# A third slot for the probabilities of attention, in the memory of the spread weights, and a wider search for TensorE's order

## The reference

```python
# layer 0: one attention head of width 128 with a causal mask, and 16 experts of width 64, two of them chosen per token
x = x + attn0(xn, R) + moe0(xn)
xn = layernorm(x)
# layer 1, first part: 16 heads of width 8, no mask
scores = einsum('bhqd,bhkd->bhqk', q, k) / sqrt(8)
ctx = einsum('bhqk,bhkd->bhqd', softmax(scores), v)
# layer 1, second part: 16 heads of width 4 on a projection to 64, causal, then 8 experts of width 256, two per token
scores = where(causal, einsum('bhqd,bhkd->bhqk', rope(q), rope(k)) / sqrt(4), -inf)
x = x + out(ctx) + moe1(x + up(softmax(scores) @ v))
```

## Time and profile before

| | before |
|---|---|
| median of 3 runs | 1917.72 us |
| lowest and highest | 1913.46 and 1918.71 us |
| the profiled execution | 1918.81 us |
| its span | 1917.0 us |
| PE, DVE, ACT, POOL busy | 1791.3, 1339.1, 1214.5, 373.6 us |
| mean granted clock of TensorE | 0.974 |

### The profile page before, as it was taken

The page is one execution under the profiler, slowest core; times in us unless marked ns, Lnnn a source line. Parts: engine busy times, 40 slices in busy tenths (PEclk is TensorE's granted clock), DMA queues, the critical chain, the costliest instruction groups (busy, mean ns, idle before and its releaser), DMA issues.

```text
span 1917.0 us, 36936 instructions
## 1 busy us (share of the span) xinstructions
PE 1791.3 (93%) x13947; PEld 810.1 (42%) x13947; DVE 1339.1 (70%) x1896; ACT 1214.5 (63%) x2347; POOL 373.6 (19%) x656
## 2 busy tenths in 40 slices
PE   6989999999898999999989999999869999999999
PEld 3664322244464322344555222344545222344656
DVE  6768698786478898775668888771545888781345
ACT  2352478888551577878542677888735688887721
POOL 2002200000045100000066000000266223300342
PEclk9999999999799999999899999999989999999999
DMA  6233610110052210110154010100174112100131
GB/s 200 73 119 90 173 29 18 29 36 3 24 168 85 61 29 18 29 36 3 33 175 124 8 29 23 31 20 14 43 198 119 32 37 63 44 20 13 44 98 56
DMA packets 97201, 117.23 MB, mean 61 GB/s; under 512 B 13048, under 2 KB 54968, under 8 KB 96768
## 3 DMA queue, kind: packets, MB, share of 16 engines
q1 hardware_dynamic: 93952, 108.58, 20.4%
q0 software_dynamic: 3072, 6.30, 1.1%
HBM read 71.67 MB, written 42.37 MB: 59 GB/s over the span
## 4 chain that ended last, share of the span: by engine, by line
PE 73%; DVE 7%; issue 5%; ACT 5%; POOL 3%; SPq 3%; DMA 2%; ACTq 0%; POOLq 0%; DVEq 0%
PE ps L2428 20%; PE ps L2398 18%; PE ps L2355 10%; PE ps L2257 4%; PE ps L2298 3%; PE ps L2287 3%; PE ps L2519 3%; ACT prob L2044 3%; DVE late_max L1819 2%; DVE row_max L1819 2%; PE ps L2342 1%; PE ps L2439 1%; PE ps L2536 1%; PE ps L2171 1%; PE ps L2214 1%
## 5 line engine op out<-in xcount | busy, mean ns | idle before, releaser
L2044 ACT ACTIVATE prob<-ps 128x512 f32<-128x512 f32 (+1 forms) x1664 | 843.9, 587 | 225.6 <-PE ps L2398 178.1
L1819 DVE TENSOR_REDUCE row_max<-ps 128x2 f32<-128x1024 f32 (+3 forms) x512 | 567.2, 1118 | 130.5 <-PE ps L2355 86.3
L2398 PE MATMUL ps<-q_stack,k_stack 80*128 80x512 bf16 (+5 forms) x1792 | 466.9, 367 | 20.9 <-ACT prob L2044 10.2
L1819 DVE TENSOR_REDUCE late_max<-ps 128x2 f32<-128x1024 f32 (+3 forms) x384 | 416.3, 1084 | 73.1 <-PE ps L2355 47.6
L2428 PE MATMUL ps<-prob,v_ones 128*32 128x512 f32 (+3 forms) x4608 | 458.1, 484 | 9.3 <-ACT prob L2044 5.5
L2355 PE MATMUL ps<-k_stack,q_stack 64*128 64x512 bf16 (+4 forms) x1792 | 306.7, 365 | 22.7 <-DMA q_stack<-scratch_rest 11.2
L2398 PEld LDWEIGHTS ps<-q_stack,k_stack 48*128 48x128 bf16 (+2 forms) x1792 | 118.9, 96 | 352.1 <-ACT prob L2044 246.9
L2355 PEld LDWEIGHTS ps<-k_stack,q_stack 64*128 64x128 bf16 (+1 forms) x1792 | 81.3, 93 | 299.4 <-DVE row_max L1819 112.6
L1979 ACT ACTIVATE prob<-ps 128x512 f32<-128x512 f32 (+1 forms) x86 | 51.2, 596 | 202.9 <-PE ps L2287 202.8
L2428 PEld LDWEIGHTS ps<-prob,v_ones 128*32 128x32 f32 x4608 | 102.1, 110 | 130.1 <-issue 59.4
L2257 PEld LDWEIGHTS ps<-wd,prob 128*128 128x128 f32 (+1 forms) x832 | 108.6, 196 | 50.0 <-issue 35.1
(11 more groups left out here) (234 smaller groups left out, 1753.5 us busy)
## 6 DMA issues: line engine op xcount, KB each, us to landing
spread_w<-scratch_r SPq DMA_DIRECT2D x128, 128.0 KB, 2.9
k_stack<-scratch_k SPq DMA_DIRECT2D x32, 256.0 KB
q_stack<-scratch_q SPq DMA_DIRECT2D x32, 256.0 KB
scratch_q<-tmp SPq DMA_DIRECT2D x8, 768.0 KB
scratch_k<-tmp SPq DMA_DIRECT2D x8, 768.0 KB
k_stack<-scratch_k SPq DMA_DIRECT2D x96, 64.0 KB
q_stack<-scratch_q SPq DMA_DIRECT2D x96, 64.0 KB
scratch_k<-tmp SPq DMA_DIRECT2D x36, 128.0 KB
```

Of the source, the lines that this page charges most:

```text
L1819: dve.tensor_reduce((nm_late if lo else nm[G % 2])[:, t, j], both, AX_X, ALU.max).then_inc(s["ring_used"], 1)
L2044: act.activation(to, src, ACT.Exp, scale=SCALES[kind_of(G)]).then_inc(s["p_ready"], 1)
L2398: ins[n] = pe.matmul(dst[n][:, to], with_rest(k_stack, G, head)[:, kc * P:(kc + 1) * P], with_rest(q_stack, G, head)[:, lo:hi], start=k == ...
```

## The change

- The four tiles of spread weights become one tile, and its memory serves as a third slot of probabilities in the window. `PROB_SLOTS` is 3. Slots go round by the quad's number inside its window.
- ACT's exponential of a quad waits for the values of the quad three before it; the first two quads of a window wait for no values, the third waits for the last multiplication with spread weights of the stretch before the window (`hid_ready`).
- SP's first four spread loads for batch 2 and 3, and the first sorted block of a batch, wait until the values of the window before are done (`pv_done`).
- The search knows of three slots, keeps 400 states instead of 100, and follows only steps that begin within 0.3 us of the earliest instead of 0.6.

```diff
--- before.py
+++ after.py
@@ -117,7 +117,8 @@
 LAT, BACK = 0.2, 0.07
 CHANGE, ISSUE = 0.093, 0.03
 ACT_TAIL, DVE_TAIL = 0.12, 0.08
-WIDTH, EVEN = 100, 0.15
+WIDTH, EVEN, SOON = 400, 0.15, 0.3
+PROB_SLOTS = 3
 POOL_FOR = (1, 2, 3)
 SILU_FOR = (1, 2, 3)
 
@@ -235,7 +236,7 @@
         starts = {}
         if c.unit < len(self.units):
             G, q, j = self.units[c.unit]
-            if G in c.ready and self.quad_of[c.unit] < c.quad + 2:
+            if G in c.ready and self.quad_of[c.unit] < c.quad + PROB_SLOTS:
                 starts["unit"] = max(c.exped[-3] + BACK, c.ready[G])
                 if in_rows("unit", G) and j % 2 == 0:
                     starts["both"] = max(c.exped[-2] + BACK, c.ready[G])
@@ -268,7 +269,7 @@
                 on_pe, on_act = self.unit_times[n]
                 end = new.on_pe("rows" if in_rows("unit", G) else "whole", (self.units[n][2] % 2,), at, on_pe)
                 quad = self.quad_of[n]
-                new.act = max(new.act, end + LAT, c.values_end[quad - 2] + LAT if quad >= 2 else 0.0) + on_act
+                new.act = max(new.act, end + LAT, c.values_end[quad - PROB_SLOTS] + LAT if quad >= PROB_SLOTS else 0.0) + on_act
                 new.exped = new.exped[1:] + (new.act + ACT_TAIL,)
             new.unit += many
             if new.unit == len(self.units) or self.quad_of[new.unit] > quad:
@@ -333,7 +334,7 @@
                         best = end, c
                     continue
                 starts = self.starts(c)
-                soon = min(max(c.issue, at) for at in starts.values()) + 0.6
+                soon = min(max(c.issue, at) for at in starts.values()) + SOON
                 for what, at in starts.items():
                     if at <= soon:
                         ahead.setdefault(done + 1 + (what == "both"), []).append(self.follow(c, what, at))
@@ -937,8 +938,17 @@
         q_stack = [sb(f"q_stack{n}", GH * S, BF16) for n in range(RING)]
         k_stack = [sb(f"k_stack{n}", GH * S, BF16) for n in range(RING)]
         prob = sb("prob", 2 * GH * HALF)
-        p_slot = lambda v, j: prob[:, (v % 2 * GH + j) * HALF:(v % 2 * GH + j + 1) * HALF]
-        p_all = prob[:].rearrange("p (v j k) -> p v j k", v=2, j=GH)
+        spread_all = sb("spread_w", SPREADS * HALF)
+        spread_w = [spread_all[:, n * HALF:(n + 1) * HALF] for n in range(SPREADS)]
+        p_slots = [prob[:, 0:GH * HALF], prob[:, GH * HALF:], spread_all[:, 0:GH * HALF]]
+
+        def in_window(G, q):
+
+            return QUAD0[G] + q - QUAD0[PER * batch_of(G)]
+
+        def p_slot(G, q):
+
+            return p_slots[in_window(G, q) % PROB_SLOTS].rearrange("p (j k) -> p j k", j=GH)
         sg, gu, hid = ([prob[:, (2 * k + n) * HALF:(2 * k + n + 1) * HALF] for n in range(2)] for k in range(3))
         spin_a, spin_b = prob[:, 6 * HALF:7 * HALF], prob[:, 7 * HALF:8 * HALF]
         heads_cT = prob[:, 6 * HALF:8 * HALF]
@@ -961,7 +971,6 @@
         mT = tmp[0][:, 0:HALF].bitcast(BF16)
         routeT = tmp[6], tmp[7]
         routes = [sb(f"routes{n}", T * EXPERTS[n]) for n in range(2)]
-        spread_w = [sb(f"spread_w{n}", HALF) for n in range(SPREADS)]
         block_hid = [sg[0][:, n * STEP1:(n + 1) * STEP1] for n in range(2)]
         block_up = [sg[1][:, n * STEP1:(n + 1) * STEP1] for n in range(2)]
         block_hidT = [gu[0][:, n * STEP1:(n + 1) * STEP1] for n in range(2)]
@@ -1251,6 +1260,8 @@
                 half, c = divmod(i, LOADS_OF // 2)
                 dst, tok = spread_w[load % SPREADS], slice(half * HALF, (half + 1) * HALF)
                 sp.wait_ge(s["routes_stored"], 16 * (routed_before(b, which) + 1))
+                if which == 0 and b >= 2 and i < SPREADS:
+                    sp.wait_ge(s["pv_done"], QUAD0[PER * (b - 1)])
                 if load >= SPREADS:
                     sp.wait_ge(s["hid_ready"], LAST_STEP[load - SPREADS] + 1)
                 if i == 0 and sorted_ahead(b, which):
@@ -1285,6 +1296,7 @@
                 if g == 0:
                     sp.wait_ge(s["scattered"], 16 * 2 * T * (b + 1))
                     sp.wait_ge(s["hid_ready"], dense_ahead(b))
+                    sp.wait_ge(s["pv_done"], QUAD0[PER * WINDOW_OF[b]])
                 before = b * SORT_GROUPS + g
                 if before >= 2:
                     sp.wait_ge(s["sx_psum"], before - 1 if g >= 2 else b * SORT_GROUPS)
@@ -2035,12 +2047,14 @@
                 v, heads = QUAD0[G] + q, units_of(kind_of(G), q)[n]
                 half, kc, lo, hi = QUADS[kind_of(G)][q]
                 act.wait_ge(s["st_psum"], u + 1)
-                if v >= 2:
-                    act.wait_ge(s["pv_done"], v - 1)
+                if in_window(G, q) >= PROB_SLOTS:
+                    act.wait_ge(s["pv_done"], v - PROB_SLOTS + 1)
+                elif in_window(G, q) == PROB_SLOTS - 1:
+                    act.wait_ge(s["hid_ready"], plan.steps_then[batch_of(G)])
                 at = half * HALF
-                to, src = p_slot(v, heads[0])[:, lo - at:hi - at], bank(UNIT_BANKS[u % 3])[:, 0:len(heads) * (hi - lo)]
+                to, src = p_slot(G, q)[:, heads[0], lo - at:hi - at], bank(UNIT_BANKS[u % 3])[:, 0:len(heads) * (hi - lo)]
                 if len(heads) == 2:
-                    to, src = p_all[:, v % 2, heads[0]::2, lo - at:hi - at], src.rearrange("p (n k) -> p n k", n=2)
+                    to, src = p_slot(G, q)[:, heads[0]::2, lo - at:hi - at], src.rearrange("p (n k) -> p n k", n=2)
                 act.activation(to, src, ACT.Exp, scale=SCALES[kind_of(G)]).then_inc(s["p_ready"], 1)
 
             def turn_max_beside(u, G):
@@ -2413,7 +2427,7 @@
                     HALVES[batch_of(how[1])] = HALVES.get(batch_of(how[1]), halves)
 
             def values(G, q, part):
-                v, kind = QUAD0[G] + q, kind_of(G)
+                kind = kind_of(G)
                 half, kc, lo, hi = QUADS[kind][q]
                 n, at = 2 * G + half, half * HALF
                 first, end = values_parts(kind, q)[part]
@@ -2425,7 +2439,7 @@
                         pe.wait_ge(s["hid_ready"], plan.steps_then[batch_of(G)])
                 pe.wait_ge(s["p_ready"], plan.quad_end[G, q])
                 for j in range(GH):
-                    ins = pe.matmul(bank(V_BANK)[CW * j:CW * (j + 1), first - at:end - at], v_st[G % 2][:, kc, j, :], p_slot(v, j)[:, first - at:end - at],
+                    ins = pe.matmul(bank(V_BANK)[CW * j:CW * (j + 1), first - at:end - at], v_st[G % 2][:, kc, j, :], p_slot(G, q)[:, j, first - at:end - at],
                                     start=kc == 0 and part == 0, stop=(half, kc) in LAST_KEYS[kind], skip_group_check=True)
                 if end == hi:
                     ins.then_inc(s["pv_done"], 1)
```

## The result

| | before | after |
|---|---|---|
| median (4 runs each, side by side) | 1917.51 us | 1890.92 us |
| lowest and highest | 1913.46 and 1918.71 us | 1886.99 and 1892.16 us |
| ratio, 95% interval | | 0.9866 [0.985, 0.9882] |
| profiled execution, its span | 1918.81, 1917.0 us | 1886.99, 1885.2 us |
| mean granted clock | 0.974 | 0.974 |

The change makes the kernel 26.6 us faster. The forecast had the direction and about 40% of the size (10.7 us against its own median), and its range ended 2 us above the result.

What follows compares the result with a forecast made beforehand. PE was taken as the bound among the plain heads, by its own work. From the profiled execution, 1918.8 - 9 - 7 + 5 + 0.5 = 1908.3 us, or 1907 as a median, with a range from 1893 to 1923.

Steps and rivals of the forecast that it cites:

- PE is the bound among the plain heads, by its own work: Plain heads in the windows: nothing waits there, so only waits at starts, among causal heads and in tails can shrink.
- Later values: Causal quads: values stand further behind their own units, so PE waits less for the last exponentials; -9 us.
- No long runs of values: Ends of causal groups: value parts stand singly between units, ACT is fed steadily, units wait less for banks; -7 us.
- More breaks: Values on PE stand in 492 runs, 470 before, and each added break costs time; +5 us, bounds 1.6 and 10.3.
- The first sorted block: Before batches 0 and 2: SP loads it only after the window's values are done; 0 to +2 us, taken +0.5.
- What costs nothing: Spread loads of batches 2 and 3 and ACT's third-quad wait: the new waits are already met, no cost.
- Rival A: Windows: PE's waits come back before units whose bank is still with ACT; 1918 us, chance 0.23.
- Rival D: The third slot isn't used, through a wait for the multiplications; 1918 us, chance 0.02.
- Rival B: Tails: a steadier tail gives back half the clock not granted, 13 us more; 1894 us, chance 0.13.
- Rival C: Causal groups and tails: breaks, lone units and sorted block cost more than waits give; 1930 us, chance 0.15.
- The signs: Plain distances stay 0.54 and 1.00 us, value-load waits under 35, windows 2 to 4 us shorter, sorted block at most 1 later.

Runs made afterwards that it cites:

- experiment 1: The change with its third slot in memory and waits, but the search planning for two slots, 100 states, 0.6 us (old order): 1916.44 us, 0.9997 of the kernel before.
- experiment 2: The kernel before, still with two slots, its search given 400 states and steps within 0.3 us: 1900.73 us, 0.9915 of the kernel before.
- experiment 5: The change with the search at 100 states instead of 400, three slots and 0.3 us kept: 1964.81 us, 1.0261 of the kernel before.

## Why the prediction was right in direction and wrong in size

- **"PE is the bound among the plain heads, by its own work … the ordering cannot remove matmuls."** This is the step that failed: the sum has no term for the plain parts, and they lost 12.7 us, nearly half of the gain and most of the 16 us by which the forecast of 1907 missed. The distances did repeat and still do, but I read only those of stretches that ran well; the old order has 53 us of waiting in the plain parts. By the table 6 to 7 us are work that moved into the causal groups, where it stands in time that was waiting before (the rest of the plain parts is 669.4 with the old order and 662.7 now, that of the causal parts 264.3 and 270.8), and about 6 us are waiting within the plain parts. Part of that is pieces that wait for VectorE's row maxima, which I had excluded: PE's idle time for them was 9.0 us in 22 waits before and is 3.7 in 7. An order cannot remove matmuls from the window, but it can from the part that is full.
- **Later values, -9 us.** The waits of value loads fell by 20.6 us. With my lower cover of 0.23 us per load, 18.7 us of before are true waiting and 33.1 - 107 x 0.23 = 8.5 of after: 10.2 us less. The idle time before values fell by 9.8 us between like traces. The term was of the right size.
- **No long runs of values, -7 us, as less idle time before units.** That idle time fell by 3.8 us between like traces (28.7 to 24.9), and by 3.0 in the causal parts and tails, where none is missing. The term was about twice too large as I defined it. What I left out is larger: 8.8 us of idle time before pieces, and the waits that show in no idle time. All in all waiting fell by 25.5 us where both terms together had 16. That ACT is fed more steadily is right. In the tail of window 2, before:

```profile
1330.88 2.31 ACT L2044 ACTIVATE prob<-ps 128x512 f32<-128x512 f32 x4 [2.52 <-PE ps L2398]
```

  and after:

```profile
1308.76 1.08 ACT L2058 ACTIVATE prob<-ps 128x512 f32<-128x512 f32 x2 [0.95 <-PE ps L2412]
```

  ACT's gap of 2.52 us is gone, and the longest of that stretch is now 0.95; over the program its idle time behind units and masks went from 219.9 to 196.9 us.
- **More breaks, +5 us.** The rest, which holds them, changed by between -5 and +3.3 us, depending on how the runs are cut, so the term was at or below its lower bound of 1.6. The Trainium skill (TensorEngine Tiling, Tiling Modes), by whose rule I would have taken 1.6, comes closer here; but the distance of 0.54 us at each pair of pieces still shows the price per change, so the runs do not say which of the two is the reason.
- **The first sorted block, +0.5 us.** Nothing. The block's turn follows the step before it by 1.89 us after window 2, as it did before (1344.63 to 1346.52 then):

```profile
1320.38 1.96 PE L2461 MATMUL ps<-const_f,v_tok 128*64 128x128 f32 x16 [0.61 <-DVE v_tok L1857]
1322.27 0.66 PE L2519 MATMUL ps<-const_f,spread_w 128*128 128x128 f32 x4
```

- **What costs nothing.** Right: experiment 1 has all of these waits and no change of time.
- **Rival A**, waits that come back at the banks, did not happen: value waits fell and idle time before units fell too, by 3.8 us between like traces. **Rival D** fell with the 9 us or more that the slot is worth.
- **Rival B**, the clock recovers, has nearly the time that was measured (1894) and is not the cause. In the tail of window 0 after the change:

```profile
480.90 0.66 PE L2412 MATMUL ps<-q_stack,k_stack 48*128 48x512 bf16 x3 [2.52 <-ACT prob L2058]
```

```profile
484.00:492.00 8.00, 8.00 (x40) 4.30 (x39) 1.22 (x1) 4.12 (x8) 0.00 (x0) 0.50 0.01 2
492.00:500.00 8.00, 8.00 (x60) 3.13 (x62) 5.48 (x19) 3.56 (x7) 0.00 (x0) 0.50 0.00 0
```

  ACT's root stands between its two table loads there, from 477.64 to 480.44, and PE idles 2.5 us as before; behind it are 16 us at the lower clock of 1.2 GHz with PE busy throughout, much as in the earlier trace rows. The mean granted clock of the kernel is 0.974 before and after.
- **Rival C** was argued in part from a false reading. I wrote that the search has no price for a change between a unit and a piece among the plain heads. It has: a piece is always of the form "rows" and a plain unit of the form "whole", so `CHANGE`, 0.093 us, is charged, and the trace's 0.10 agrees. The mechanism on the other side that does exist, I did not see: an order for three slots that pushes the maxima behind other transfers on SP. It is what a narrower search gets, +0.8% and +2.6%, and a look at SP's list in the new order would have shown that it is not there inside the windows.
- **The parts of the change.** I put the gain down to the third slot, which allows values to come later. Added to the new search, the slot is worth 9.4 of the 26.6 us; added to 400 states with the old bound, 18. The bound of 0.3 us, which I gave no term at all, brings 0.7% alone and 0.85% with 400 states, without the slot.
- **The signs.** The distances stayed, the waits of value loads fell below 35 us (33.1), the sorted block did not come later. The windows did not shrink by 2 to 4 us each but by 8, 4, 7 and 4, and the tail of window 1 did not shrink at all (31.3 us before, 32.8 after, with more of it at the lower clock, see the last section). One reading was wrong and changed nothing: the earlier trace rows has PE busy 282 us in the second window and 277 in the third, so it does do more there.

What stays open: why a strict bound finds the better order. The runs show where the time goes, not which of the search's choices do it. Whether a longer search with the stacks held back beats the change was not tried.

## What to carry to other kernels

- Before you call an engine the bound in a stretch, compare every repeated pattern with its quickest copy, over the whole stretch, and add up the idle time of all its products. Waits that are shorter than the modelled end of the product before them never show as idle time; here they were some 6 of 20 us in the causal parts and tails.
- Before you compare idle time in two traces, compare the number of records. 90 missing products of 1792 made 14 us of idle time that was not there; set against the complete trace of before, they hid 14 of the 22 us that had gone.
- More buffers do nothing until the order uses them (0.9997), and an order that is allowed to run further ahead may push small urgent transfers behind large ones on a queue (2 of 2.6%). Look at each queue's list, not only at the engines'.
- When a change has a resource and a search in it, try each alone and both. Here the search alone gave 0.85% of 1.34%, the resource alone nothing, and the resource with half of the search 1.0%.

## What was not expected of the hardware

- The lower clock does not follow how much PE idles in a stretch. With two slots and the new search (experiment 2) window 1's tail keeps 0.94 on average with PE idle 4 of 29 us; with the change it falls to 0.74 with PE idle 3 of 33. In the first (upper rows) the half clock takes part of one stretch, in the second a whole one and parts of both its neighbours:

```profile
896.00:904.00 8.00, 5.59 (x83) 3.11 (x81) 3.46 (x19) 7.17 (x14) 0.00 (x0) 1.00 0.01 2
904.00:912.00 8.00, 7.37 (x51) 3.69 (x55) 2.76 (x8) 5.54 (x12) 1.17 (x2) 0.79 0.00 1
912.00:920.00 8.00, 7.17 (x85) 3.94 (x78) 4.14 (x13) 5.93 (x13) 0.00 (x0) 1.00 0.01 2
```

```profile
888.00:896.00 8.00, 5.41 (x46) 2.33 (x35) 2.34 (x9) 7.67 (x14) 1.17 (x2) 0.80 0.00 0
896.00:904.00 8.00, 8.00 (x44) 4.70 (x46) 1.26 (x2) 2.44 (x5) 0.00 (x0) 0.50 0.00 1
904.00:912.00 8.00, 7.88 (x75) 2.20 (x72) 5.68 (x19) 5.39 (x11) 0.00 (x0) 0.64 0.01 2
```

  The wait before it is the same, 2.57 and 2.52 us, behind the same square root. The tail is 32.8 us long with the change and 29.1 in experiment 2; how much of these 3.7 us is the clock was not measured by itself.
- Issues on SP's queue take their time one by one: the eight for the stacks in experiment 5 took 5.2 us, from 263.60 to 268.76, and the small transfer behind them went out 3.6 us later than with the stacks held back (265.19). PE's wait for it was 2.06 us there.
